# Second attention's prologue reordered: the second batch's front in a bank of its own beside the first batch's, its stacks between the first batch's scores

## The reference

```python
q = split_heads(x)                                  # 16 heads of 8
k = split_heads((x @ w_dk + b_dk) @ w_uk + b_uk)
v = split_heads((x @ w_dv + b_dv) @ w_uv + b_uv)
q, k = _apply_rope(q, cos, sin), _apply_rope(k, cos, sin)
attn = softmax(einsum('bhid,bhjd->bhij', q, k) / sqrt(8))
x = _layernorm(x + (attn @ v) @ w_o + b_o)
```

## Time and profile before

| | us |
|---|---|
| median of 3 runs | 1535.35 |
| lowest, highest | 1532.27, 1535.51 |
| the profiled execution's own time | 1534.11 |
| its span | 1532.3 |
| busy: PE, DVE, ACT, POOL | 1373.3, 1020.5, 916.6, 642.3 |
| second attention's prologue, first instruction to first scores of `batches` | 866.7 to 928.68 |
| `batches`, to about | 1288 |

### The profile page before, as it was taken

How to read it: one execution, slowest core, us unless ns; L and a number is a source line. 1 busy time by engine, 2 the same in 40 slices (tenths; PEclk the granted TensorE clock), 3 DMA queues, 4 the chain that set the end, 5 groups by cost and what they waited for, 6 DMA issues and landing times. The chain is left out here.

```text
span 1532.3 us, 34933 instructions
## 1 busy us (share of the span) xinstructions
PE 1373.3 (90%) x10621; PEld 1111.5 (73%) x10622; DVE 1020.5 (67%) x3322; ACT 916.6 (60%) x2484; POOL 642.3 (42%) x975
## 2 busy tenths in 40 slices
PE   5999999999999999589999568999999999898946
PEld 4777777777777777478888446778787877676934
DVE  4777777777777777556666656888888887472213
ACT  3666666666666666345555325676767676695823
POOL 1344444444444444413333422244444432333772
PEclk9999999999999999889999758999999999998988
DMA  6111111111111110011111422220223200007935
GB/s 233 42 51 45 53 44 54 41 57 43 55 44 54 44 54 7 13 43 46 49 45 48 128 73 71 71 74 29 69 83 101 96 10 13 15 15 223 282 99 171
DMA packets 64179, 106.95 MB, mean 70 GB/s; under 512 B 11616, under 2 KB 49632, under 8 KB 61616
## 3 DMA queue, kind: packets, MB, share of 16 engines
q1 hardware_dynamic: 49728, 84.41, 17.9%
q0 software_dynamic: 8864, 18.43, 3.4%
q10 hardware_dynamic: 5520, 3.28, 0.7%
HBM read 85.57 MB, written 61.60 MB: 96 GB/s over the span
## 5 line engine op out<-in xcount | busy, mean ns | idle before, releaser
L369 POOL TENSOR_TENSOR a_prob<-a_prob,a_rl 128x128 f32<-128x128 f32 (+1 forms) x256 | 124.5, 507 | 239.7 <-DVE a_rl L458 239.2
L253 ACT ACTIVATE a_prob<-psum,a_nmx 128x128 f32<-128x128 f32 (+1 forms) x512 | 210.7, 423 | 11.0 <-DVE a_nmx L453 11.0
L2010 DVE TENSOR_REDUCE a_mx<-psum 128x2 f32<-128x512 f32 x256 | 170.6, 688 | 42.5 <-PE psum L1342 40.3
L281 ACT ACTIVATE a_probt<-psum 128x768 f32<-128x768 f32 x128 | 103.8, 811 | 128.2 <-PE psum L705 128.2
L1702 ACT ACTIVATE a_prob<-psum 128x1024 f32<-128x1024 f32 x128 | 129.2, 1024 | 13.3 <-PE psum L1374 12.8
L452 DVE TENSOR_REDUCE a_nmx<-psum 128x2 f32<-128x256 f32 x128 | 54.3, 425 | 118.9 <-PE psum L641 118.8
L835 POOL DMA_INDIRECT yt<-m_yrow,m_dest x71 | 67.9, 956 | 146.0 <-DVE m_yrow L955 144.6
L294 ACT ACTIVATE a_ot<-psum,a_bias 128x256 f32<-128x256 f32 x128 | 61.4, 480 | 93.0 <-PE psum L729 93.0
L1342 PE MATMUL psum<-a_k_stk,q_stk 128*128 128x256 f32 x512 | 112.1, 318 | 2.8 <-DVE a_mx L2010 2.1
L705 PE MATMUL psum<-ident,a_prob 128*128 128x128 f32 x768 | 106.1, 274 | 8.8 <-DVE a_prob L462 7.7
L253 ACT ACTIVATION_READ_ACCUMULATOR a_prob<-psum,a_nmx 128x1 f32 x512 | 107.6, 210 | 0.0
(11 more groups left out here) (345 smaller groups left out, 4099.1 us busy)
## 6 DMA issues: line engine op xcount, KB each, us to landing
xs<-in_fill SPq DMA_DIRECT2D x144, 264.0 KB
m_w<-in_wr SPq DMA_DIRECT2D x39, 321.0 KB, 4.1
a_stage<-in_w SPq DMA_DIRECT2D x16, 384.0 KB, 4.2
m_xrow<-xs SPq DMA_DIRECT2D x39, 132.0 KB, 3.8
m_xrow<-xs SPq DMA_DIRECT2D x71, 66.0 KB, 1.8
a_yin<-yt SPq DMA_DIRECT2D x16, 256.0 KB, 2.7
f_yin<-yt SPq DMA_DIRECT2D x8, 512.0 KB, 4.6
yt<-m_yrow,m_dest POOLq DMA_INDIRECT x149, 2.2
```

The source lines that it names most:

```text
L253: last = nc.scalar.activation(prob[:, slot, h, at], S[:, 2 * slot + h, at], ACT.Exp, bias=nmx[:, slot, q, h:h + 1], accum_out=lsum[:, slot ...
L281: nc.scalar.activation(probt[:, hp % 2], PT[:, :, 0:SW], ACT.Copy).then_inc(pt_done, 1)
L369: last = nc.gpsimd.tensor_tensor(prob[:, slot, 0, at], prob[:, slot, 0, at], rl[:, slot, 0, q:q + 1].to_broadcast(prob[:, slot, 0, at].sha ...
L2010: nc.vector.reduce_max(mx[:, :, h:h + 1], bank.rearrange("p (q k) -> p q k", q=QB), AX.X).then_inc(mx_done, 1)
```

## The change

The matmuls, copies and sums are the same in number, shape and engine. What changes is their order in the prologue, and the banks that some of them use.

- The second batch's incoming rows, latents, keys and turned keys go to bank PV in place of MISC, and come much earlier: incoming rows behind the first batch's keys, latents behind its turned keys, keys between its stacks 1 and 2, `turn` behind its stack 3. On DVE both rotations of the second batch are done before the first maximum.
- The second batch's stacks 0, 1 and 2 go to three of the banks ST, behind the first batch's first scores 3, 5 and 7.
- The third batch's incoming rows, latents and keys are done behind first scores 9, 12 and 15.
- POOL does the second batch's part of the rotation and weighs the third batch's rows before it splits the shared experts' weights.
- DVE's six constants move from the front's start to behind the first batch's turned maxima.

PE's order, then DVE's, cut to the prologue's own list (the helpers only gain a `bank` argument, which the second batch's calls set to PV or a bank of ST):

```diff
             latents(columns_of(0), 1)
             keys(columns_of(0), 1)
+            incoming(2, PV)
             pe.wait_ge(k_done, 1)
             pe.wait_ge(xsin_done, 1)
             values(0)
             turn()
+            pe.wait_ge(rx_done, 2)
+            latents(columns_of(1), 2, PV)
             pe.wait_ge(sel_done, 1)
             pe.wait_ge(q_split, 1)
             pe.wait_ge(k_split, 1)
             stack(0, R0)
             stack(1, R1)
+            keys(columns_of(1), 2, PV)
             pe.wait_ge(stack_act, 1)
             stack(2, R0)
             pe.wait_ge(stack_dve, 1)
             stack(3, R1)
-            pe.wait_ge(v_done, 1)
-            pe.wait_ge(ksin_done, 1)
-            incoming(2)
+            pe.wait_ge(k_done, 2)
+            pe.wait_ge(xsin_done, 2)
+            turn(PV)
             pe.wait_ge(stack_act, 3)
             for h in range(H1):
                 if h >= 2:
                     pe.wait_ge(mx_done, h - 1)
                 first_scores(h, 0, (R0, R1)[h % 2])
                 if h == 3:
-                    pe.wait_ge(rx_done, 2)
-                    latents(columns_of(1), 2)
+                    pe.wait_ge(q_split, 2)
+                    pe.wait_ge(k_split, 2)
+                    stack(0, ST[:, 0, :])
+                if h == 5:
+                    stack(1, ST[:, 1, :])
                 if h == 7:
-                    keys(columns_of(1), 2)
-            pe.wait_ge(k_done, 2)
-            pe.wait_ge(xsin_done, 2)
-            turn()
+                    stack(2, ST[:, 2, :])
+                if h == 9:
+                    pe.wait_ge(v_done, 1)
+                    pe.wait_ge(ksin_done, 2)
+                    incoming(3)
+                if h == 12:
+                    pe.wait_ge(rx_done, 3)
+                    latents(columns_of(2), 3)
+                if h == 15:
+                    keys(columns_of(2), 3)
             maxima(1)
-            pe.wait_ge(q_split, 2)
-            pe.wait_ge(k_split, 2)
-            stack(0, R0)
-            pe.wait_ge(mt_done, 1)
-            stack(1, R1)
-            pe.wait_ge(stack_act, 4)
-            stack(2, R0)
-            pe.wait_ge(ksin_done, 2)
-            incoming(3)
-            pe.wait_ge(rx_done, 3)
-            latents(columns_of(2), 3)
-            keys(columns_of(2), 3)
+            pe.wait_ge(stack_act, 5)
             pe.wait_ge(stack_dve, 2)
...
             incoming_low(columns_of(0), 1)
+            incoming_variances(2)
...
+            incoming_rows(2)
             rotate_q_first(1)
             rotate_q_rest(1)
+            incoming_low(columns_of(1), 2, PV)
             rotate_k_first(1)
             values(0, 1)
             rotate_k(1)
             stacks(1, 0, 1)
-            incoming_variances(2)
-            incoming_rows(2)
+            rotate_q_first(2, PV)
+            dve.wait_ge(stack_ps, NGR)
+            rotate_q_rest(2)
+            rotate_k_first(2, PV)
+            rotate_k(2)
             for h in range(H1):
                 maxima(h, (R0, R1)[h % 2], 1)
+                if h == 1:
+                    incoming_variances(3)
                 if h == 3:
-                    incoming_low(columns_of(1), 2)
+                    incoming_rows(3)
                 if h == 7:
-                    rotate_q_first(2)
+                    stacks(1, 1, 2, ST[:, 1, :])
+                if h == 11:
+                    incoming_low(columns_of(2), 3)
             negate(1)
-            rotate_q_rest(2)
-            rotate_k_first(2)
-            rotate_k(2)
             turned_maxima(0, 1)
...
-            stacks(1, 1, 2)
-            incoming_variances(3)
-            incoming_rows(3)
-            incoming_low(columns_of(2), 3)
             rotate_q_first(3)
```

More of the change, by code:

```diff
@@ L1327, in values, with turn @@
                 last.then_inc(v_ps, 1)
-            def turn():
-                nc.tensor.matmul(MISC[:, T:2 * T], small32[:, 2, :], k32[:], start=True, stop=True).then_inc(turn_ps, 1)
+            def turn(bank=MISC):
+                nc.tensor.matmul(bank[:, T:2 * T], small32[:, 2, :], k32[:], start=True, stop=True).then_inc(turn_ps, 1)
             def stack(k, bank):
@@ L1419, in tail_store, with incoming @@
                 last.then_inc(ntr_ps, 1)
-            def incoming(n):
+            def incoming(n, bank=MISC):
                 pe.wait_ge(rows_done, n)
                 for q in range(QB):
-                    last = nc.tensor.transpose(MISC[:, q * P:(q + 1) * P], rows[:, q, :], g.ident[:])
+                    last = nc.tensor.transpose(bank[:, q * P:(q + 1) * P], rows[:, q, :], g.ident[:])
                 last.then_inc(rtr_ps, 1)
@@ L1682, in _, with latents, keys @@
         def _(act):
-            def latents(p, n):
+            def latents(p, n, bank=MISC):
                 act.wait_ge(lat_ps, n)
-                nc.scalar.activation(klat[:], MISC[:, 0:T], ACT.Identity, bias=bias[:, 0:1])
-                nc.scalar.activation(vlat[:, p, :], MISC[:, T:2 * T], ACT.Identity, bias=bias[:, 1:2]).then_inc(lat_done, 1)
-            def keys(n):
+                nc.scalar.activation(klat[:], bank[:, 0:T], ACT.Identity, bias=bias[:, 0:1])
+                nc.scalar.activation(vlat[:, p, :], bank[:, T:2 * T], ACT.Identity, bias=bias[:, 1:2]).then_inc(lat_done, 1)
+            def keys(n, bank=MISC):
                 act.wait_ge(k_ps, n)
-                nc.scalar.activation(k32[:], MISC[:, 0:T], ACT.Identity, bias=bias[:, 2:3]).then_inc(k_done, 1)
+                nc.scalar.activation(k32[:], bank[:, 0:T], ACT.Identity, bias=bias[:, 2:3]).then_inc(k_done, 1)
             def stacks(k, p, bank, n):
@@ L1719, in tail_store, with incoming @@
                 nc.scalar.activation(g.xth[:, at], MISC[:, 0:T], ACT.Copy).then_inc(nt_act, 1)
-            def incoming(at, n):
+            def incoming(at, n, bank=MISC):
                 act.wait_ge(rtr_ps, n)
-                nc.scalar.activation(g.xth[:, at], MISC[:, 0:T], ACT.Copy).then_inc(rt_act, 1)
+                nc.scalar.activation(g.xth[:, at], bank[:, 0:T], ACT.Copy).then_inc(rt_act, 1)
             def router(n, bank):
@@ L1739, in _ @@
             keys(1)
+            incoming(columns_of(1), 2, PV)
+            latents(1, 2, PV)
             stacks(0, 0, R0, 1)
+            keys(2, PV)
             stacks(2, 0, R0, 1)
             stacks(3, 0, R1, 1)
[L1743 to L1747, removed]
+            stacks(0, 1, ST[:, 0, :], 2)
+            stacks(2, 1, ST[:, 2, :], 2)
             incoming(columns_of(2), 3)
@@ L1980, in rotate_rest, with rotate_q_first @@
                                         ).then_inc(signal[2], 1)
[L1982 removed]
+            def rotate_q_first(n, bank=MISC):
                 dve.wait_ge(k_done, n)
[L1984 removed]
+                rotate_first(bank[:, T:2 * T], xsin, xsin_done)
             def rotate_q_rest(n):
@@ L2123, in _ @@
             incoming_low(columns_of(0), 1)
+            incoming_variances(2)
+            dve.wait_ge(sel_in, 16)
+            nc.vector.tensor_copy(sel[:].rearrange("p a k n -> p (a k n)"),
+                                  prob[:].rearrange("p a h t -> p (a h t)")[:, 0:H1 * P]).then_inc(sel_done, 1)
+            incoming_rows(2)
+            rotate_q_first(1)
+            rotate_q_rest(1)
+            incoming_low(columns_of(1), 2, PV)
+            rotate_k_first(1)
+            values(0, 1)
+            rotate_k(1)
+            stacks(1, 0, 1)
+            rotate_q_first(2, PV)
+            dve.wait_ge(stack_ps, NGR)
+            rotate_q_rest(2)
+            rotate_k_first(2, PV)
+            rotate_k(2)
+            for h in range(H1):
+                maxima(h, (R0, R1)[h % 2], 1)
+                if h == 1:
+                    incoming_variances(3)
+                if h == 3:
+                    incoming_rows(3)
+                if h == 7:
+                    stacks(1, 1, 2, ST[:, 1, :])
+                if h == 11:
+                    incoming_low(columns_of(2), 3)
+            negate(1)
+            turned_maxima(0, 1)
             nc.vector.tensor_copy(ident_r[:], g.ident[:])
```

52 lines of the change are left out of this document (17 added, 35 removed).

## The result

| | before | changed |
|---|---|---|
| median, us | 1535.22 (4 runs) | 1523.99 (4 runs) |
| lowest, highest | 1532.27, 1535.51 | 1523.53, 1527.12 |
| profiled execution, its span | 1534.11, 1532.3 | 1527.12, 1525.3 |

The ratio is 0.9926, with a 95% interval of 0.9911 to 0.994: 11.2 us less by the medians, where 10.5 were forecast.

The account below looks back on a forecast made before the run. No engine was taken to bound the prologue, only a chain of short steps between engines; PE bounds the loop. Terms of -14.1, +3.2 and +0.4 sum to -10.5 us, giving 1524.2 us, range 1519.8 to 1529.3.

Parts of the forecast that it names:

- 1, tail behind the last maximum: From the last maximum to the first scores of `batches`: 1.8 us in place of 15.9, 14.1 saved.
- 2, the keys' split: First batch's front: POOL's weighing holds up DVE's split of the keys, so the first stack starts 1.05 us later.
- 3, first maximum, term 2 included: From stacks to first maximum: POOL's weight instructions hold up DVE's second rotation; first maximum 3.2 us later in all.
- 4, length of the maxima: First batch's maxima with added DVE work and stacks between: 16.4 us for 15.94, 0.4 more.
- rival B: POOL does not block DVE in the prologue, or comes second: 14.1 us saved, 1520.6; chance 0.09.
- The granted clock should be 0.50 up to `batches`: Sign in the profile: PE's clock stays at half speed through the prologue and rises within 6 us of `batches`' start.
- rival A: Clock rises in the prologue: maxima 1.5 us less, start of `batches` up to 2 less, 1521 to 1522.5; chance 0.19.
- the forecast case: The kernel's time lands between 1522.5 and 1526.5 us; chance 0.56.
- Edits at nothing: DVE's moved six constants and SP's earlier loads and clearing cost nothing; uncovered, the constants would cost half a microsecond.
- Rivals C: Overlap in the maxima fails, stacks and DVE's additions add up: gain only 5.4 us, 1529.3; chance 0.09.
- D: Gain given back: `batches` waits for clearing DMAs or loads that haven't moved, 1534.7; chance 0.04.
- E: Slower: the clock rises later in `batches`, 27 us more at half clock giving about 1538; chance 0.03.

Follow-up runs that it names:

- c2: The changed kernel with POOL's split of the shared experts' weights moved behind its weighing of the fourth batch's rows: 1522.10 us, ratio 0.9907.
- c3: c2 plus one wait: POOL weighs the third batch's rows only after the first batch's keys are split: 1519.37 us, ratio 0.9886.
- c4: The changed kernel with POOL's second weight instruction done twice: 1525.84 us, ratio 0.9935.
- c1: The changed kernel run again as it stands: 1524.54 us, ratio 0.9915 to the kernel before.
- c7: c3 with small unread matmuls filling PE's pauses up to the first scores of `batches`: 1519.71 us, ratio 0.9894.
- c9: The changed kernel once more, on a third chip where the kernel before takes 1568.04 us: 1555.13 us, ratio 0.9914.
- c10: c3 once more, on a third chip where the kernel before takes 1568.04 us: 1550.45 us, ratio 0.9888.
- c6: The changed kernel with the third batch's incoming rows, latents and keys moved behind the first batch's turned maxima: 1526.15 us, ratio 0.9937.
- c5: The changed kernel with the second batch's stacks 0, 1 and 2 moved behind the first batch's turned maxima: 1522.49 us, ratio 0.9919.
- c8: The kernel before with small unread matmuls filling PE's pauses up to the first scores: 1533.90 us, ratio 0.9993.

## Why the prediction was right

By its own terms, from T in the two first profiles:

| term | forecast | measured |
|---|---|---|
| 1, tail behind the last maximum | -14.1 | -14.2 (15.91 to 1.69) |
| 2, the keys' split | +1.05 | +1.22 |
| 3, first maximum, term 2 included | +3.2 | +3.6 |
| 4, length of the maxima | +0.4 | -1.0 (15.94 to 14.93) |
| prologue | -10.5 | -11.6 |
| the loop | 0 | -1.2 |

**Terms 1 to 3 held**, and so did their mechanism. The reading of the cast beside POOL's sum carried two terms, and c2, c3 and c4 move each of them on its own: take the weights away, 2.4 to 2.7 us less to the first maximum; let the weighing wait, 1.2 less to the split keys; double the second instruction, 2.1 to 2.3 more. The Trainium skill's rule ("SBUF — State Buffer", section "Who interferes with whom"), that the later of the two blocks for the whole instruction, agrees with the cast of 2.34 us in the change and with c4's subtraction of 2.51. Without it the change would have been forecast 3 us too fast, rival B. Its 3.6 us are a price of this order, not of the idea, since c3's kernel has them back.

**Term 4 and the clock were wrong.** "The granted clock should be 0.50 up to `batches`" failed, and "some 16.4 us for the maxima" with it. These windows of the changed kernel show it (columns as in the earlier trace rows):

```profile
900.00:901.00 1.00, 0.78 (x2) 0.06 (x1) 1.00 (x1) 1.00 (x4) 1.00 (x1) 0.64 0.00 0
...
904.00:905.00 1.00, 0.00 (x0) 0.00 (x0) 0.85 (x3) 0.00 (x0) 0.00 (x0) 0.57 0.00 0
910.00:911.00 1.00, 1.00 (x6) 0.81 (x5) 1.00 (x4) 0.82 (x3) 0.59 (x1) 0.52 0.00 0
...
917.00:918.00 1.00, 0.92 (x7) 0.92 (x8) 0.63 (x2) 0.00 (x0) 0.81 (x2) 0.90 1.17 304
...
921.00:922.00 1.00, 0.78 (x5) 0.26 (x3) 0.48 (x4) 0.47 (x1) 0.02 (x1) 0.90 0.00 0
```

It rises at 900.7, behind 6 us of unbroken matmuls from 894.73, the first place that rival A named; it falls at 904.1, as the pauses there made me expect; it rises again at 911, behind the scores and stacks from 906.70 on, a place that rival A did not name; it is low once more from 917.8 to 921.2, and up when `batches` begins at 922.58. There, from 911 on, it shortens the scores that DVE waits for: four take 1.10 us at 914.87, where they took 1.39 at 906.70.

In the term's own words, DVE's 13.4 us of work between the first and the last maximum were right (13.65), and the 3.0 us of its waits for PE were the mistake: they were 1.3. Eight profiles have this same work there (the change, c1 to c4, c7, c9 and c10). DVE waits least where the clock was at 1.00 for some 9 us of it (c1 and c3: 1.0 and 0.9 us, maxima of 14.6 and 14.5), and most where it was so for 3.4 (c4: 2.2 us, 16.0); the five others (14.9 to 15.5) lie between, not in strict order. The level of the clock is thus what the term lacked. No run had it low throughout with the stacks in place, so the 16.4 themselves are not tested. The size of rival A, 1.5 us in the maxima and up to 2 in `batches`, was about right: 1.4 and 1.2. It came together with the forecast case, not in place of it.

**The loop** shows the same thing. Over the ten profiles ahead of c9 its length is 359.3 to 359.7 us where no time is spent at half clock, and longer with that time, by about 0.37 us for each us (360.8 at 3.9, 361.5 at 5.6). I had priced it at 0.5. An exception is c6, 359.8 at 1.7, at some 0.2.

**The medians** moved 11.2 us, though the second attention alone is 12.8 shorter in the profiles (11.6 and 1.2). T itself differs from execution to execution, 877.2 to 883.6 over these ten profiles. The clock near the start of the program goes with it, as one window of the kernel before and of the change's first profile shows:

```profile
28.00:32.00 4.00, 4.00 (x37) 2.99 (x36) 2.92 (x9) 3.01 (x12) 0.52 (x2) 1.00 0.28 112
28.00:32.00 4.00, 4.00 (x23) 2.35 (x21) 1.09 (x3) 1.62 (x5) 0.39 (x1) 0.50 0.30 118
```

It is 0.50 there in the three profiles with T over 883 (the first, c1 and c7), about 0.65 in c3 and c6 (880.6 and 880.9), and 1.00 in the kernel before and in c2, c4, c5 and c8 (877.2 to 879.0). No kernel differs in that part of the program, so it is chance that the change's first profile had it low. No run tests it as the cause of a late T.

**Edits at nothing.** The six constants cost 0.35 us: PE waits so long for the third batch's sine product before the values at 923.88 in the timeline above. Half a microsecond had been the price without cover.

**Rivals C, D and E** are out: the maxima did not get longer, the loop's end moved with its start, and the clock was up when `batches` began. **Rival B** is out by the cast of 2.34 us.

## What to carry to other kernels

A start-up chain in which no engine is the bound costs the length of its serial part: look for idle banks (what the banks give by themselves no run here shows), so that the second item's chain can run inside the first one's pauses. When steps move between engines, write down beside each VectorE cast and two-input sum what GpSimd does at that moment; one long GpSimd instruction that starts just ahead of a short, critical one can cost nearly its whole length (2.34 us for a cast of 0.29, beside 2.43), and beside VectorE's reads of PSUM it cost nothing that shows (in c3, with the two weight instructions beside them, four maxima took 2.57 us, as in the change without). And compare profiles from a point inside the program ahead of which nothing differs: run to run noise here was half the effect.

## What the runs showed of the hardware

- The clock's level differs between executions of one kernel. In the changed kernel's three profiles it rose to 1.00 at 17.1, 14.1 and 9.5 us behind T (the first, c1 and c9), in c9 during PE's pause ahead of the first stack. In the first profile it fell at 917.8 although PE's longest pause since the rise at 911 was 1.34 us (before 914.87).
- Filling PE's pauses raised the clock in the front and moved the first maximum by 1.7 us (c7 against c3, c8 against the kernel before), but the total by nothing that the runs can tell. In both the clock was down again when the PE-bound loop began, for 3.8 and 2.7 us.
- A GpSimd instruction of 0.72 to 2.43 us on SBUF held up the VectorE cast, sum or subtraction that started behind it until 0.15 to 0.3 us behind its end, and did so to a second one in a row when the GpSimd instruction was doubled (c4).
